# Turning a group's queries by DMA instead of by identity matmuls in a two-layer gated cross-attention kernel

## Chip, core and metric

The kernel runs on one core of a Trainium2 chip. The metric is the device time of one execution in microseconds (us), lower is better. The engines are named as in the profile: PE (TensorE matmuls) and PEld (its weight loads), DVE (VectorE), ACT (ScalarE), POOL (GpSimd) and SP (SyncE, which here only issues DMAs).

## What is computed

The input has 4 sequences of 256 tokens of width 256 and a context of 1601 rows each. Layer 0 is attention with two kinds of queries, a feed-forward part with eight experts follows, and layer 1 has another cross-attention and a product with weights made of bits. The change is in layer 0's attention, of which this is the core of the reference:

```
q  = _ln(linear_fp8(ln_out, wq ).reshape(b, s, g, hpg, d), qln_w,  qln_b)
k  = _ln(linear_fp8(ln_out, wk ).reshape(b, s, g, d), kln_w, kln_b)
core = _gqa(q, k, v)                       # over the 256 own tokens
qx = _ln(linear_fp8(ln_out, wqx).reshape(b, s, g, hpg, d), qxln_w, qxln_b)
xout = _gqa(qx, kx, vx)                    # over the 1601 context rows
catq = div_clamp_fp8(concat([core, xout]), proj_smooth)
out  = catq @ wproj.T * (proj_in_scale * proj_w_scale)
```

There are g = 8 groups with hpg = 2 heads of d = 128 each, so that a kind of query of one group and one sequence is 2 x 2 blocks (128 tokens x 128 features). `_ln` normalises over the 128 features of a head and then multiplies by a weight and adds a bias for each feature.

## The kernel before

**Turns.** Layer 0's attention is a loop of 32 turns, one for each pair of group and sequence (`NGB`, the variable `it`). Every engine runs an order written out by hand in a loop over `it` of its own (`pe_attention`, `act_attention`, `dve_attention`, `pool_attention`, `sp_attention`), with semaphores between them. In turn `it` the scores and the softmax of four blocks n = 4*it to 4*it+3 are made, while keys, queries and values of turn it+1 are prepared, and the products with V and the projection of earlier turns are finished. A score block n takes two steps on PE, `scores(n, 0)` and `scores(n, 1)` (L1810).

**Precision.** The two operands of each attention product are held as two bf16 tiles, an upper part and what it leaves (the lower part), and multiplied in three matmuls.

**Queries.** For each kind (i = 0 the cross kind, i = 1 the own kind) PE makes a block of 128 tokens x 512 (L1763, `queries`); DVE takes the statistics (L1249, L1255); POOL makes scale and shift (L1083 to L1088); ACT normalises four blocks into `kn` (L1509). PE then turns them, so that features lie on partitions, with four fp32 identity matmuls (L1774, `turn_queries`, two kinds a turn), since the scores need them so. ACT applies weight and bias, which are now per partition, while it reads PSUM (L1521, `query_full`, into `t32`, shown as `t`). POOL rounds to bf16 (L1097) and makes the lower part (L1099) in `QT` (`query_low`). `scores(4*it, 0)` and `scores(4*it, 1)` wait for these.

**Key row.** PE sums the keys' squares (L1711), ACT sends them to `ssc` (L1530, L1534), POOL takes their power in `key_norm` (L1108), and SP writes the row to memory (`row_out`, L987) and reads it back broadcast over the partitions (`row_in`, L1000, 936 KB, into `rsb` in odd turns and into `x` in even ones). DVE multiplies each score block by it (L1289).

**Probabilities.** ACT takes exponentials (L1555, L1556) and writes the upper part `PB` (L1565, `p_hi`), DVE the lower part (L1311, `p_lo`), POOL those of the own tokens (L1125, L1127, L1129, `split_self`). SP then turns each block of them by two transposing DMAs (L1015, `turn_p(n, h)`: half h = 0 is 16 tiles of 128 x 128 in bf16, half h = 1 is 14), eight a turn, and PE multiplies by V (L1830, `times_v`). `p_hi(n, h)` may write its half of `PB` only when that half of block n-2 has landed.

**SP's order in a turn.** Weights for later turns (L970) and pieces of other inputs; then `turn_p(4*it, 1)`, `turn_p(4*it, 0)`, `turn_p(4*it+1, 0)`; the key row out and in; the projection's weights (L978, 512 KB); `turn_p(4*it+1, 1)` and the last four `turn_p` of the turn. All DMAs of SP share one queue, whose 16 engines serve it in order.

## Times and profile before

| | |
|---|---|
| median of 3 runs | 1680.82 us (1679.46 to 1682.97) |
| profiled execution, first to last instruction | 1678.0 us |
| attention loop of layer 0, first to last score matmul | 61.0 to 1145.8 us |
| PE busy over the whole span | 1597.7 us, 95% |
| DVE, ACT, POOL busy | 1389.4, 1387.6, 1130.8 us |
| DMA queue of SP | 258.05 MB, 71.3% of 16 engines' time |

The profile has no time of its own for the profiled execution beside its span; the median of the plain runs is 2.8 us above that span, and this part (launch and end) is outside what the trace shows. In the profile's slices a digit is a busy share in tenths. A DMA share can exceed 1, since packets of one DMA engine overlap. In rows of the timeline a merged group's start and length are given, and in brackets the idle time ahead of it and what ended it.

### The profile page before, as it was taken

The page shows a single profiled execution, that of the slowest core. Times are in us where ns is not written, and L with a number is a line of the kernel's source. Part 1 is how long each engine was busy: PE and PEld are TensorE (multiplying, and loading weights), DVE is VectorE, ACT ScalarE, POOL GpSimd, SP SyncE. Part 2 cuts the span into 40 slices and gives each one's busy share as a digit, 9 for nine tenths or more (in the row PEclk, how much of TensorE's full clock was granted, in tenths as well). Part 3 has the DMA queues.
Part 4 walks back from the last instruction along what each step waited for, and adds up shares of the span by engine and source line. Part 5 has one row for each costly group of instructions (what it writes and reads, how often), then busy time and mean ns, then how long its engine had stood idle before and what let it go on. Part 6 is the DMA issues. An engine that isn't in the chain of part 4 may idle for free. (4 is left out here: it accounts for less than half of the span.)

```text
span 1678.0 us, 44059 instructions
## 1 busy us (share of the span) xinstructions
PE 1597.7 (95%) x15996; PEld 1003.1 (60%) x15996; DVE 1389.4 (83%) x3489; ACT 1387.6 (83%) x2340; POOL 1130.8 (67%) x1766
## 2 busy tenths in 40 slices
PE   3799999999999999999999999997898999999998
PEld 1476777767777677777777777765564333333333
DVE  7889999999999989999988999999896755655422
ACT  6688888888887888888887887876347999999997
POOL 3568778687787877888787878875575655646300
PEclk9799999999999999999999999998999999999999
DMA  5299989899989998999999999999323222222100
GB/s 179 85 200 204 195 196 198 188 203 208 211 193 202 223 206 187 213 223 220 206 198 215 220 220 192 201 189 237 95 48 115 46 46 74 45 40 46 33 14 14
DMA packets 608904, 261.11 MB, mean 156 GB/s; under 512 B 576560, under 2 KB 581680, under 8 KB 607280
## 3 DMA queue, kind: packets, MB, share of 16 engines
q1 hardware_dynamic: 604464, 258.05, 71.3%
q8 instruction: 127, 2.08, 0.5%
q10 hardware_dynamic: 4224, 0.25, 0.2%
q14 instruction: 89, 0.73, 0.1%
HBM read 99.15 MB, written 17.29 MB: 69 GB/s over the span
## 5 line engine op out<-in xcount | busy, mean ns | idle before, releaser
L1810 PE MATMUL score<-KK,QT 128*128 128x512 bf16 (+2 forms) x1920 | 341.8, 322 | 7.4 <-DVE mxp L1289 7.3
L1830 PE MATMUL pv<-PT,VV 128*128 128x256 bf16 (+1 forms) x2880 | 335.7, 273 | 6.1 <-DMA PT<-PB 6.1
L1565 ACT ACTIVATE PB<-S,rsum 128x1024 bf16<-128x1024 f32 (+1 forms) x256 | 246.3, 988 | 105.5 <-DVE rsum L1320 79.6
L1830 PEld LDWEIGHTS pv<-PT,VV 128*128 128x128 bf16 (+1 forms) x2880 | 278.3, 98 | 70.8 <-issue 31.6
L1311 DVE SCALAR_TENSOR_TENSOR PB<-S,rsum,PB 128x1024 bf16<-128x1024 f32 (+1 forms) x256 | 291.1, 1138 | 0.0
L1810 PEld LDWEIGHTS score<-KK,QT 128*128 128x128 bf16 x1920 | 157.9, 98 | 145.3 <-DVE mxp L1289 14.5
L1555 ACT ACTIVATE S<-S,nmx 128x1601 f32<-128x1601 f32 x128 | 210.1, 1641 | 3.6 <-DVE nmx L1301 3.5
L2870 ACT ACTIVATE P<-score 128x1024 f32<-128x1024 f32 x196 | 198.0, 1054 | 1.7 <-PE score L2962 0.8
L1689 PE MATMUL tb<-stage,wsb 128*128 128x512 bf16 (+1 forms) x768 | 149.5, 337 | 5.2 <-DVE stage L643 3.9
L2982 PE MATMUL pv<-P,V 128*9 128x256 f32 (+1 forms) x2288 | 152.2, 380 | 1.1 <-DVE pv L2253 0.8
L1125 POOL TENSOR_SCALAR S<-S,rsum 128x256 f32<-128x256 f32 x128 | 72.2, 564 | 115.3 <-DVE rsum L1320 107.4
L1147 POOL TENSOR_TENSOR catq<-yt,ym 128x512 bf16<-128x512 f32 x64 | 116.1, 1813 | 0.3
L1289 DVE CUSTOM_DVE_ANT_0 S<-score,x 128x1024 f32<-128x1024 f32 (+1 forms) x128 | 104.5, 816 | 7.5 <-PE score L1810 5.5
L1289 DVE CUSTOM_DVE_ANT_0 S<-score,rsb 128x1024 f32<-128x1024 f32 (+1 forms) x128 | 104.5, 816 | 6.7 <-PE score L1810 2.9
L1689 PEld LDWEIGHTS tb<-stage,wsb 128*128 128x128 bf16 x768 | 66.5, 98 | 71.3 <-issue 8.5
L1137 POOL TENSOR_TENSOR yt<-yq,ym 128x512 f32<-128x512 bf16 x64 | 94.8, 1482 | 12.8 <-DVE ym L1345 8.3
L1730 PE MATMUL tb<-wsb,stage 128*128 128x128 bf16 x1536 | 99.7, 223 | 3.0 <-DVE KK L1222 2.8
L1509 ACT ACTIVATE kn<-pa,a_nm,a_rs 128x128 f32<-128x128 f32 x256 | 95.5, 454 | 8.1 <-POOL a_nm L1088 8.0
L1083 POOL TENSOR_SCALAR a_nm<-a_mv 128x4 f32<-128x4 f32 x64 | 41.7, 651 | 89.3 <-DVE a_mv L1255 89.3
L1730 PEld LDWEIGHTS tb<-wsb,stage 128*128 128x128 bf16 x1536 | 94.1, 100 | 7.2 <-DVE KK L1222 5.2
L1481 ACT ACTIVATE KK<-tb,dcols 128x512 bf16<-128x512 f32 (+1 forms) x128 | 76.1, 594 | 25.7 <-PE tb L1689 25.7
L1129 POOL TENSOR_TENSOR PB<-S,PB 128x256 bf16<-128x256 f32 x128 | 89.3, 698 | 10.9
(293 smaller groups left out, 3679.6 us busy)
## 6 DMA issues: line engine op xcount, KB each, us to landing
x<-rs_d SPq DMA_DIRECT2D x16, 936.0 KB, 5.0
rsb<-rs_d SPq DMA_DIRECT2D x16, 936.0 KB, 5.6
wsb<-w_split SPq DMA_DIRECT2D x46, 256.0 KB, 4.7
wsb<-w_split SPq DMA_DIRECT2D x23, 512.0 KB, 4.8
wpr<-in_wprojT SPq DMA_DIRECT2D x23, 512.0 KB, 6.5
context_d<-stage SPq DMA_DIRECT2D x16, 400.2 KB, 3.8
l_ctx<-context_d SPq DMA_DIRECT2D x4, 1601.0 KB, 7.8
rawh<-in_w_all SPq DMA_DIRECT2D x12, 512.0 KB, 5.8
```

Source lines behind the costliest of these rows:

```text
L1147: e.tensor_tensor(out[:, :, pr * 256:(pr + 1) * 256], m.yt[:, :].rearrange("p (k c) -> p k c", k=2), m.ym[pr][:, :].rearrange("p (k c) -> ...
L1289: e.tensor_tensor_reduce(m.S32[par][:, at:at + b - a], m.score[:, a:b], m.rsb[it % 2][:, key:key + b - a], 1.0, start, ALU.mult, ALU.max, ...
L1311: e.scalar_tensor_tensor(m.PB[n % 2][:, lo:lo + b - a], m.S32[n % 2][:, a:b], m.rsum[n % 2][:, 1:2], m.PB[n % 2][:, 2 * a:a + b], ALU.mult ...
L1509: a = e.activation(m.kn[i][:, k * D:(k + 1) * D], bank[:, k * D:(k + 1) * D], ACT.Identity, bias=m.anm[i][:, k:k + 1], scale=m.ars[i][:, k ...
L1555: e.activation(x, x, ACT.Exp, bias=m.nmx[par][:, 1:2], accum_out=m.sums[par][:, 1:2])
L1565: e.activation(m.PB[n % 2][:, 2 * a:a + b], m.S32[n % 2][:, a:b], ACT.Copy, scale=m.rsum[n % 2][:, 1:2]).then_inc(s["p_hi"], 1)
L1689: r = e.matmul(bank[:, 0:b - a], wk[:, w, ic, D:2 * D], ctx_op(m, it, part, ic, a, b), start=(n == 0), stop=(n == 5))
L1730: r = e.matmul(bank[:, h * D:(h + 1) * D], ctx_op(m, it, part, ic, t * P, (t + 1) * P), wv[:, w, ic, D:2 * D], start=(n == 0), stop=(n == 5))
L1810: i = e.matmul(m.score[:, at:at + b - a], qt[:, kind, qp, q * P:(q + 1) * P], kk[:, kp, a:b], start=(k == 0), stop=(k == 2))
L1830: i = e.matmul(m.pv[:, at:at + 256], vv[0:rows, v, t, :], m.PT[k % 2][0:rows, turned(c, a), :], start=(c == first and r == 0), stop=(c == ...
L2870: e.activation(pr[:, :], bank, ACT.Exp, scale=float(D1) ** -0.5).then_inc(s["l1_exp"], 1)
L2982: r = e.matmul(m.pv[j * R:j * R + VC, 0:S], m.V1[p][0:rows, t, 4 * hq + j, :], probabilities(m, n, j // 2)[0:rows, at:at + S], start=(t == ...
```

## The change

The eight identity matmuls of a turn go, and ACT's pass with weight and bias over PSUM with them. Weight and bias now lie along the free dimension (`qrow`, the four vectors broadcast to all partitions by one DMA at the start), and POOL applies them to `kn` in two instructions (`query_weighted`). ACT writes the upper part in bf16 (`query_high`), POOL the lower part (`query_low`), both into `q16`, and SP turns upper and lower part of a kind in one transposing DMA of 8 tiles (`turn_q`) into `QT`. `kn` is one buffer instead of two. The slots of PSUM banks that the turned queries had are left empty.

```diff
@@ -193,8 +193,9 @@
             m.wsb = sb(c, "wsb", [P, 2 * IC * WCOLS], BF16)
             m.sq = sb(c, "sq", [P, SQG * SQW], F32)
             m.sqs = sb(c, "sqs", [P, SQW], F32)
-            m.kn = [sb(c, f"kn{i}", [P, 512], F32) for i in range(2)]
-            m.t32 = sb(c, "t32", [P, 512], F32)
+            m.kn = sb(c, "kn", [P, NQ, D], F32)
+            m.qrow = sb(c, "qrow", [P, 4, D], F32)
+            m.q16 = sb(c, "q16", [P, 2, NQ * D], BF16)
             qt, kk, vv = [None, None], [None, None], [None, None]
             qt[0] = sb(c, "QT0", [P, 2, 2, NQ * P], BF16)
             kk[0] = sb(c, "KK0", [P, 2, KCOLS], BF16)
...
@@ -506,6 +507,7 @@
     e.dma_start(m.cols[:, :], A["cols"]).then_inc(s["const_in"], 16)
     e.dma_start(m.dcols[:, :], A["dcols"]).then_inc(s["const_in"], 16)
     e.dma_start(m.scal[:, :], A["scal"].partition_broadcast(P)).then_inc(s["const_in"], 16)
+    e.dma_start(flat(m.qrow[:, :, :]), A["qrow"].partition_broadcast(P)).then_inc(s["const_in"], 16)
     e.dma_start(m.smc[:, :], A["smooth"]).then_inc(s["const_in"], 16)
     sp_load_weights(e, m, s, 0)
     sp_load_context(e, m, s, 0, 0)
...
@@ -838,8 +840,8 @@
 
 
 
-SLOTS = (("Q0",), ("K0",), ("K1",), ("TQ0",), ("K2",), ("K3",), ("Q1",), ("SS",), ("V0",), (), ("V1",), ("TQ1",), ("V2",),
-         ("V3",), ("PR",))
+SLOTS = (("Q0",), ("K0",), ("K1",), (), ("K2",), ("K3",), ("Q1",), ("SS",), ("V0",), (), ("V1",), (), ("V2",), ("V3",),
+         ("PR",))
 ORDER = tuple(w for slot in SLOTS for w in slot)
 SLOT = {w: n for n, slot in enumerate(SLOTS) for w in slot}
 LAG = 3
...
@@ -1014,6 +1014,15 @@
             e.wait_ge(s["tv_done"], 2 * (k - 2) + h + 1)
         e.dma_start_transpose(m.PT[k % 2][:, 2 * a // P:2 * b // P, (n % 2) * P:(n % 2 + 1) * P],
                               m.PB[n % 2][:, 2 * a:2 * b]).then_inc(s[f"pt{h}_in{n % 2}"], 16)
+
+    def turn_q(it, i):
+        if not it < NGB:
+            return
+        e.wait_ge(s["q_lo"], 2 * it + i + 1)
+        if it >= 2:
+            e.wait_ge(s["bank_full"], 8 * (it - 1))
+        e.dma_start_transpose(m.QT[it % 2][:, 1 - i, :, :].rearrange("p a (k q) -> p (a k) q", q=P),
+                              flat(m.q16[:, :, :])).then_inc(s["qt_in"], 16)
 
     for it in range(-1, NGB + LAG - 1):
         if it == -1:
...
@@ -1045,6 +1054,7 @@
         load_weights(it + 2, 0)
         if it + 2 >= PAIRS:
             load_weights(it + 2, 1)
+        turn_q(it + 1, 0)
         turn_p(4 * it, 1)
         turn_p(4 * it, 0)
         turn_p(4 * it + 1, 0)
...
@@ -1056,6 +1066,7 @@
             load_projection(it - 1)
         if it == NGB - 1:
             load_projection(NGB - 1)
+        turn_q(it + 1, 1)
         turn_p(4 * it + 1, 1)
         if it == NGB - 2:
             load_projection(it - 1)
...
@@ -1087,17 +1098,25 @@
         e.wait_ge(s["rs_pow"], 2 * c + 2)
         e.tensor_tensor(m.anm[i][:, :], m.anm[i][:, :], m.ars[i][:, :], ALU.mult).then_inc(s["nm_done"], 1)
 
+    def query_weighted(it, i):
+        if not it < NGB:
+            return
+        c, w = 2 * it + i, 2 * (1 - i)
+        if c == 0:
+            e.wait_ge(s["const_in"], 80)
+        e.wait_ge(s["normed"], c + 1)
+        e.tensor_tensor(m.kn[:, :, :], m.kn[:, :, :], m.qrow[:, w:w + 1, :].broadcast_to([P, NQ, D]),
+                        ALU.mult).then_inc(s["q_t32"], 1)
+        e.wait_ge(s["q_t32"], 2 * c + 1)
+        e.tensor_tensor(m.kn[:, :, :], m.kn[:, :, :], m.qrow[:, w + 1:w + 2, :].broadcast_to([P, NQ, D]),
+                        ALU.add).then_inc(s["q_t32"], 1)
+
     def query_low(it, i):
         if not it < NGB:
             return
-        c, kind = 2 * it + i, 1 - i
-        e.wait_ge(s["q_t32"], c + 1)
-        if it >= 2:
-            e.wait_ge(s["bank_full"], 8 * (it - 1))
-        e.tensor_copy(m.QT[it % 2][:, kind, 0, :], m.t32[:, :]).then_inc(s["q_hi"], 1)
+        c = 2 * it + i
         e.wait_ge(s["q_hi"], c + 1)
-        e.tensor_tensor(m.QT[it % 2][:, kind, 1, :], m.t32[:, :], m.QT[it % 2][:, kind, 0, :],
-                        ALU.subtract).then_inc(s["q_lo"], 1)
+        e.tensor_tensor(m.q16[:, 1, :], flat(m.kn[:, :, :]), m.q16[:, 0, :], ALU.subtract).then_inc(s["q_lo"], 1)
 
     def key_norm(it):
         if not it < NGB:
...
@@ -1151,18 +1170,19 @@
         if it == 0:
             e.wait_ge(s["xq_done"], 8)
             for i in range(2):
-                e.memset(m.S32[i][:, SC:SELFC], 0.0).then_inc(s["p_pad"], 1)
+                e.memset(m.S32[i][:, SC:SELFC], 0.0).then_inc(s["set_zero"], 1)
         query_norm(it + 1, 0)
         take_magnitudes(2 * it - 3)
         split_self(4 * it - 1)
+        query_weighted(it + 1, 0)
         if it < NGB - 1:
             projection_low(it - 2)
         if it == -1:
             pool_context_low(e, m, s, 1, 0)
             pool_context_low(e, m, s, 1, 1)
+        query_low(it + 1, 0)
         split_self(4 * it)
         query_norm(it + 1, 1)
-        query_low(it + 1, 0)
         if it == -1:
             pool_split_weights(e, m, s, 1, 0)
             pool_round_end(e, m, s, 4)
...
@@ -1170,11 +1190,12 @@
         if 0 <= it < SPLITS and it % 2 == 0:
             pool_split_weights(e, m, s, it // 2 + 2, 1)
         split_self(4 * it + 1)
+        query_weighted(it + 1, 1)
         key_norm(it + 1)
         if it == -1:
             pool_round_end(e, m, s, 5)
+        query_low(it + 1, 1)
         add_magnitudes(2 * it - 2)
-        query_low(it + 1, 1)
         if it == -1:
             pool_round_end(e, m, s, 6)
         if it == NGB - 4:
...
@@ -1503,23 +1524,21 @@
             return
         bank = bank_of(m, f"Q{i}")
         e.wait_ge(s["nm_done"], 2 * it + i + 1)
-        if it:
-            e.wait_ge(s["pa_full"], made(it - 1, f"TQ{i}"))
+        if it or i:
+            e.wait_ge(s["q_lo"], 2 * it + i)
         for k in range(NQ):
-            a = e.activation(m.kn[i][:, k * D:(k + 1) * D], bank[:, k * D:(k + 1) * D], ACT.Identity,
+            a = e.activation(m.kn[:, k, :], bank[:, k * D:(k + 1) * D], ACT.Identity,
                              bias=m.anm[i][:, k:k + 1], scale=m.ars[i][:, k:k + 1])
         a.then_inc(s["normed"], 1)
 
-    def query_full(it, i):
+    def query_high(it, i):
         if not it < NGB:
             return
-        c, kind = 2 * it + i, 1 - i
-        w = ("qln", "qxln")[kind]
-        e.wait_ge(s["pa_full"], made(it, f"TQ{i}"))
+        c = 2 * it + i
+        e.wait_ge(s["q_t32"], 2 * c + 2)
         if c:
-            e.wait_ge(s["q_lo"], c)
-        e.activation(m.t32[:, :], bank_of(m, f"TQ{i}")[:, :], ACT.Identity, scale=dcol(m, w + "_w"),
-                     bias=dcol(m, w + "_b")).then_inc(s["q_t32"], 1)
+            e.wait_ge(s["qt_in"], 16 * c)
+        e.copy(m.q16[:, 0, :], flat(m.kn[:, :, :])).then_inc(s["q_hi"], 1)
 
     def sums_out(it):
         if not it < NGB:
...
@@ -1592,7 +1611,7 @@
                 act_norm_weighted(e, m, s, ic)
             act_scaled_inputs(e, m, s, 4)
         exponentials(4 * it)
-        query_full(it + 1, 0)
+        query_high(it + 1, 0)
         for j in SCALES_AT.get(it, ()):
             act_scaled_inputs(e, m, s, j)
         act_piece_high(e, m, s, it, "A")
...
@@ -1641,7 +1660,7 @@
             for what, c in ffn_slots(0):
                 act_prepare(e, m, s, 0, what, c)
         values_high(it + 1, 1)
-        query_full(it + 1, 1)
+        query_high(it + 1, 1)
         act_piece_high(e, m, s, it, "D")
         if 0 <= it < SPLITS:
             act_weights_high(e, m, s, it // 2 + 2, 3 * (it % 2))
...
@@ -1764,16 +1783,6 @@
                              wq[:, w, ic, kind * 256:(kind + 1) * 256], start=(n == 0), stop=(n == 3))
         r.then_inc(s["pa_full"], 1)
 
-    def turn_queries(it, i):
-        if not it < NGB:
-            return
-        bank = bank_of(m, f"TQ{i}")
-        wait_bank(e, s, it, f"TQ{i}")
-        e.wait_ge(s["normed"], 2 * it + i + 1)
-        for k in range(NQ):
-            r = e.transpose(bank[:, k * P:(k + 1) * P], m.kn[i][:, k * D:(k + 1) * D], m.ident[:, :])
-        r.then_inc(s["pa_full"], 1)
-
     def project(i):
 
         if not 0 <= i < NGB:
...
@@ -1798,7 +1807,7 @@
         if q == 0:
             if half == 0:
                 e.wait_ge(s["k_lo"], 4 * it + 4)
-            e.wait_ge(s["q_lo"], 2 * it + 1 + half)
+            e.wait_ge(s["qt_in"], 16 * (2 * it + 1 + half))
         if n and half == 0:
             e.wait_ge(s["mm"], 3 * (n - 1) + 1)
         elif n:
...
@@ -1841,7 +1850,6 @@
             pe_turn_normed(e, m, s, 1)
         scores(4 * it + 1, 0)
         times_v(2 * it - 2, 1)
-        turn_queries(it + 1, 0)
         scores(4 * it + 1, 1)
         keys(it + 1, 2)
         keys(it + 1, 3)
...
@@ -1864,7 +1872,6 @@
         if it != NGB - 1:
             scores(4 * it + 2, 1)
         values(it + 1, 1)
-        turn_queries(it + 1, 1)
         values(it + 1, 2)
         values(it + 1, 3)
         scores(4 * it + 3, 0)
...
@@ -3110,6 +3117,7 @@
     names = ["ln_w", "ln_b", "q_in_scale", "qx_in_scale", "k_in_scale", "v_in_scale"]
     out["cols"] = np.ascontiguousarray(np.concatenate([l0(n).reshape(IC, P).T for n in names], axis=1))
     out["dcols"] = np.ascontiguousarray(np.stack([l0(n) for n in DCOLS], axis=1))
+    out["qrow"] = np.concatenate([l0(n) for n in ("qln_w", "qln_b", "qxln_w", "qxln_b")])
     out["scal"] = np.concatenate([z.reshape(-1) for z in (
         l0("wq_scale"), l0("wqx_scale"), l0("wk_scale"), l0("wv_scale"), l0("proj_w_scale"), l0("proj_in_scale"),
         a["g_xattn"], a["g_ffn"], a["L1_ffn_scale"], a["L1_ffn_biasscale"])])
```

On SP, this is one turn before, from the key row of one turn to the last transposes ahead of the next one (`rs_d<-rr` is the row out, `PT<-PB` a `turn_p`).

```order
L987 DMA rs_d<-rr 128x15 [waits rs_in0,kr_pow]
L1000 DMA x<-rs_d 128x1872 [waits mm,rs_row]
L978 DMA wpr<-in_wprojT 128x1024 [waits pw_lo]
L1015 DMA_TRANSPOSE PT<-PB 128x14x128 [waits tv_done,s_lo,p_lo]
L1015 DMA_TRANSPOSE PT<-PB 128x16x128 [waits tv_done,p_lo]
```

And the same place in the changed program.

```order
L987 DMA rs_d<-rr 128x15 [waits rs_in0,kr_pow]
L1000 DMA x<-rs_d 128x1872 [waits mm,rs_row]
L978 DMA wpr<-in_wprojT 128x1024 [waits pw_lo]
L1024 DMA_TRANSPOSE QT<-q 128x8x128 [waits bank_full,q_lo]
L1015 DMA_TRANSPOSE PT<-PB 128x14x128 [waits tv_done,s_lo,p_lo]
L1015 DMA_TRANSPOSE PT<-PB 128x16x128 [waits tv_done,p_lo]
```

The own kind's queries (i = 1) are turned behind the key row and the projection's weights and ahead of the last five `turn_p`. Also on SP, this is the place before between the last `turn_p` of one turn and the first ones of the next.

```order
L1015 DMA_TRANSPOSE PT<-PB 128x14x128 [waits tv_done,s_lo,p_lo]
L970 DMA wsb<-w_split 128x1024 [waits pa_full]
L484 DMA stage<-inputs_d 128x2048 [waits xq_out1,xq_out0,ctx_lo_dve]
L970 DMA wsb<-w_split 128x1024 [waits pa_full]
L970 DMA wsb<-w_split 128x2048 [waits pa_full]
L1015 DMA_TRANSPOSE PT<-PB 128x14x128 [waits tv_done,s_lo,p_lo]
```

And in the changed program.

```order
L970 DMA wsb<-w_split 128x1024 [waits pa_full]
L485 DMA stage<-inputs_d 128x2048 [waits xq_out1,xq_out0,ctx_lo_dve]
L970 DMA wsb<-w_split 128x1024 [waits pa_full]
L970 DMA wsb<-w_split 128x2048 [waits pa_full]
L1024 DMA_TRANSPOSE QT<-q 128x8x128 [waits bank_full,q_lo]
L1015 DMA_TRANSPOSE PT<-PB 128x14x128 [waits tv_done,s_lo,p_lo]
```

The cross kind's queries (i = 0) are turned behind the weights and ahead of `turn_p(4*it, 1)`.

On POOL, this is the stretch before from the second query's statistics to the magnitudes (`a_nm`, `a_rs` are shift and scale, `S`, `PB` the own tokens' probabilities, `rr` the key row).

```order
L1088 TENSOR_TENSOR a_nm<-a_nm,a_rs 128x4 [waits rs_pow]
L1097 CAST QT<-t 128x512 [waits bank_full,q_t32]
L1099 TENSOR_TENSOR QT<-t,QT 128x512 [waits q_hi]
L1125 TENSOR_SCALAR S_1<-S_1,rsum 128x256 [waits pt1_in1,sum_read]
L1127 CAST PB<-S_1 128x256 [waits s_hi]
L1129 TENSOR_TENSOR PB<-S_1,PB 128x256 [waits s_hi]
L1108 TENSOR_TENSOR rr<-ssc,mhalf 128x15 [waits rs_row,sums_in]
L1137 TENSOR_TENSOR yt<-yq,ym 128x512 [waits yq_done,y_mag]
L1097 CAST QT<-t 128x512 [waits bank_full,q_t32]
L1099 TENSOR_TENSOR QT<-t,QT 128x512 [waits q_hi]
```

And the same stretch of the changed program.

```order
L1099 TENSOR_TENSOR a_nm<-a_nm,a_rs 128x4 [waits rs_pow]
L1144 TENSOR_SCALAR S_1<-S_1,rsum 128x256 [waits pt1_in1,sum_read]
L1146 CAST PB<-S_1 128x256 [waits s_hi]
L1148 TENSOR_TENSOR PB<-S_1,PB 128x256 [waits s_hi]
L1108 TENSOR_TENSOR kn<-kn,qrow 128x512 [waits normed]
L1111 TENSOR_TENSOR kn<-kn,qrow 128x512 [waits q_t32]
L1127 TENSOR_TENSOR rr<-ssc,mhalf 128x15 [waits rs_row,sums_in]
L1119 TENSOR_TENSOR q<-kn,q 128x512 [waits q_hi]
L1156 TENSOR_TENSOR yt<-yq,ym 128x512 [waits yq_done,y_mag]
```

The two new instructions of the own kind stand ahead of the key row's power, and the cross kind's cast and lower part no longer stand in this stretch (its new ones are earlier in the turn).

## Rows read from the trace of the kernel before

**Rows 1.** The page: busy time of the engines, DMA share in 40 slices.

```profile
PE 1597.7 (95%) x15996; PEld 1003.1 (60%) x15996; DVE 1389.4 (83%) x3489; ACT 1387.6 (83%) x2340; POOL 1130.8 (67%) x1766
DMA  5299989899989998999999999999323222222100
```

**Rows 2.** Busy time by stretch: length, PE, PEld, DVE, ACT, POOL, PEclk, DMA share, GB/s.

```profile
306.90:343.00 36.10, 35.91 (x324) 25.95 (x323) 34.19 (x86) 30.13 (x57) 27.91 (x32) 1.00 0.95 198
818.30:852.35 34.05, 34.05 (x314) 25.06 (x313) 30.09 (x80) 28.15 (x53) 27.39 (x31) 1.00 0.97 206
920.50:954.55 34.05, 34.05 (x315) 25.06 (x313) 31.68 (x82) 28.36 (x51) 28.18 (x31) 1.00 1.02 219
```

**Rows 3.** Timeline of PE, 818 to 863 us: start, length, line, out<-in, count.

```profile
818.54 1.46 PE L1810 MATMUL score<-KK,QT 128*128 128x512 bf16 x6
...
842.42 0.60 PE L1774 MATMUL tb<-ident,kn 128*128 128x128 f32 x4
842.86 1.50 PE L1730 MATMUL pa<-wsb,stage 128*128 128x128 bf16 x24
...
852.59 1.46 PE L1810 MATMUL score<-KK,QT 128*128 128x512 bf16 x6
...
855.19 1.24 PE L1810 MATMUL score<-KK,QT 128*128 128x512 bf16 x9
```

**Rows 4.** The page's groups of POOL: count, busy us, mean ns, idle before.

```profile
L1137 POOL TENSOR_TENSOR yt<-yq,ym 128x512 f32<-128x512 bf16 x64 | 94.8, 1482 | 12.8 <-DVE ym L1345 8.3
L1099 POOL TENSOR_TENSOR QT<-t,QT 128x512 bf16<-128x512 f32 x64 | 76.9, 1201 | 5.2
L1097 POOL CAST QT<-t 128x512 bf16<-128x512 f32 x64 | 42.9, 670 | 0.2 <-issue 0.2
```

**Rows 5.** Timeline of POOL, 838 to 848 us.

```profile
841.72 2.75 POOL L1108 TENSOR_TENSOR rr<-ssc,mhalf 128x15 f32<-128x15 f32 x1
...
846.63 1.16 POOL L1099 TENSOR_TENSOR QT<-t,QT 128x512 bf16<-128x512 f32 x1
```

**Rows 6.** Timeline of ACT, 821 to 858 us.

```profile
821.34 0.69 ACT L1481 ACTIVATE KK<-tb,dcols 128x512 bf16<-128x512 f32 x1 [0.35 <-PE tb L1689]
...
838.80 1.48 ACT L1509 ACTIVATE kn<-pa,a_nm,a_rs 128x128 f32<-128x128 f32 x4
...
857.39 0.84 ACT L1565 ACTIVATE PB<-S,rsum 128x640 bf16<-128x640 f32 x1
```

**Rows 7.** Timeline of SP, 831 to 872 us: a length is how long SP was held by the issue.

```profile
831.08 2.14 SPq L970 DMA_DIRECT2D wsb<-w_split  x2
837.03 7.85 SPq L1015 DMA_TRANSPOSE PT<-PB  x3
844.98 0.98 SPq L987 DMA_DIRECT2D rs_d<-rr  x1
847.57 0.32 SPq L1000 DMA_DIRECT2D rsb<-rs_d  x1
...
848.47 14.39 SPq L1015 DMA_TRANSPOSE PT<-PB  x5
```

**Rows 8.** DMAs issued at 847.57 and 848.47 us: size, us from issue to landing.

```profile
rsb<-rs_d SPq DMA_DIRECT2D x1, 936.0 KB, 6.1
PT<-PB SPq DMA_TRANSPOSE x1, 8.2
```

**Rows 9.** The `turn_p(4*it+1, 1)` issued at 917.56 us: us to landing.

```profile
PT<-PB SPq DMA_TRANSPOSE x1, 9.0
```

**Rows 10.** Busy time by stretch, columns as in Rows 2.

```profile
836.50:838.00 1.50, 1.50 (x15) 1.34 (x14) 1.37 (x2) 0.82 (x2) 1.34 (x4) 1.00 0.24 98
...
846.50:848.50 2.00, 2.00 (x20) 1.61 (x19) 1.81 (x5) 1.01 (x6) 1.22 (x2) 1.00 0.16 25
...
853.00:864.60 11.60, 11.60 (x83) 7.16 (x82) 10.08 (x28) 9.64 (x17) 8.95 (x10) 1.00 1.15 227
...
869.50:872.00 2.50, 2.50 (x24) 1.55 (x24) 2.28 (x5) 1.36 (x5) 2.20 (x5) 1.00 0.21 74
```

28 lines of the change are left out of this document (13 added, 15 removed).

## The prediction

> **What bounds the kernel now.** I read the page first. PE is busy 95% of the span, and the DMA engines stand at 9 tenths in most slices of the attention loop [rows 1]. Then the busy time by stretch. In the two turns from 818 and from 920 us PE is busy all of 34.05 us at full clock, VectorE 30 to 32, ScalarE 28, GpSimd 27 to 28, and the DMA share is 0.97 and 1.02 [rows 2]. So PE sets these turns: one goes from the score matmul at 818.54 to that at 852.59 [rows 3], 34.05 us. Some turns are different: in 306.9 to 343.0 PE and VectorE (34.19 of 36.10) are both nearly full [rows 2]. By the same reading five of the 32 turns are held by VectorE. I call the others PE's; the early ones among them take some 0.4 us more than 34.05 and get the same treatment.
>
> **What goes.** Four identity matmuls run from 842.42 to the next block at 842.86 [rows 3]: 0.44 us (their length of 0.60 overlaps what follows). Two kinds a turn make 0.88 us, and 32 turns 28.2 us. The trace shows no idle PE in these turns to swallow that. ScalarE's pass with weight and bias becomes a copy of the same 128x512, no dearer; I cost this edit at nothing, since ScalarE has 6 us free a turn [rows 2]. The floor is therefore 1680.8 - 28.2 = 1652.6 us, with a PE turn of 33.17.
>
> **What comes on GpSimd.** Per kind two 128x512 operations in fp32 come and one cast of 0.67 goes; the lower part of 1.20 stays. No row has two fp32 inputs and an fp32 output at this width. The nearest are 1.20 (fp32 and bf16 in) and 1.48 (fp32 out) [rows 4]; I take 1.25, the inputs counting more, with both as ends. That is 2 x (2 x 1.25 - 0.67) = 3.7 us a turn (3.5 to 4.6): GpSimd goes from 27 or 28 to 31 or 32 of 34 us [rows 2], still below PE. What matters is where they stand. The key row's power ran at 841.72 to 844.47 [rows 5]. In the new order it stands behind the own kind's two operations, which wait for ScalarE's normalised block at 838.80 + 1.48 = 840.28 [rows 6]: 840.3 + 2.5 + 2.75 = 845.5, so 1.1 us later. SP issued the row at 844.98 [rows 7], so its issue slips by 0.6. Half of this is hidden, for the row out can only land behind the transposes already queued; I take 0.3 us for the row's return. The lower part then ends at 845.5 + 1.2 = 846.7, before SP comes to it at 848.47 [rows 7].
>
> **What comes on the DMA queue.** Two transposes of 8 tiles. Their rate is that of the busy stretch 853.0 to 864.6, at 227 GB/s [rows 10]: 128 x 1024 x 2 bytes = 262 KB take 1.15 us; the five `turn_p` there are 74 tiles in 11.6 us [rows 7, 10], or 1.25 for 8 tiles. I take 1.2 each, 2.4 a turn. A table of the Trainium skill (VectorE: DVE Perf Modes, "Rules for kernel authors") says to turn a 128x128 tile on TensorE if PSUM will do as the place, and by DMA otherwise, at 1309 ns a tile by DMA. That rule speaks against this change. By its figure 16 tiles would be an estimated 21 us a turn, but here 8 tiles take 1.2, so the figure is that of a lone tile and the sum goes by the rows.
>
> *The cross kind* is issued while SP waits: its last load is out at 833.2 and the next `turn_p` goes at 837.03 [rows 7]. The DMA engines are at 0.24 from 836.5 to 838 and at 0.21 from 869.5 to 872 [rows 10]. There it costs nothing. In turns with more loads this gap is full, and all behind it comes up to 1.2 us later.
>
> *The own kind* stands behind the key row, which lands at 847.57 + 6.1 = 853.7, and behind the projection's weights. `turn_p(4*it+1, 1)` landed at 848.47 + 8.2 = 856.7 from that place [rows 7, 8]. It has 14 tiles, so 8 tiles would land 6 x 0.15 = 0.9 earlier, at 855.8. PE wants them for the second half of the first score block at 855.19 [rows 3]: 0.6 us too late. In the turn with the 917.56 issue the landing took 9.0 [rows 9], to 926.6, less 0.9 is 925.7. PE's time there is 855.19 plus two turns, 923.29: 2.4 late. I take 1.2 for a mean over turns, plus 0.3 for the row, plus 0.3 for filled gaps: 1.8 us.
>
> **Three loops that must shorten for a gain.** (a) Queries. The chain to this landing starts at ScalarE's run from 821.34, which follows PE's first keys [rows 6], ahead of the place where PE would now wait. A late landing so delays the chain only through the turn after, and two turns share it: period = 34.05 + (1.8 - 0.88)/2 = 34.5. With 0.6 late in place of 1.8 it is 33.9; with 2.4 + 0.3 + 1.2 it is 35.6. (b) Probabilities. `turn_p(4*it+1, 1)` landed at 856.7 and ScalarE writes that buffer again at 857.39 [rows 6]: 0.7 in hand. In the other turn it landed at 926.6, where ScalarE wants it at 857.39 plus two turns, 925.5: 1.1 late, and PE was still full from 920.5 on [rows 2, 9]. So 1.8 is in hand at least. It gets 1.2 + 0.3, and up to 1.2 more: 33.8 to 35.0. (c) The queue itself. From 836.5 to 872 it is idle in three places: 1.1 us, 1.7 us and 2.0 us [rows 10]. The first and the last are the same place of two turns, so one counts. The 1.7 us is the round trip of the key row, for which SP waits, and stays. So some 2.0 of a light turn can be filled, and 2.4 come: 34.4. All three centre on 34.4 or above, and none comes near 33.17.
>
> **Sum.** I take 34.45, that is +0.4 us for 24 turns (+9.6), nothing for the five of VectorE, and the full gain for three at the edges (-2.6): +7. Against the profiled span of 1678.0 that is 1685, against the median 1688. Measurement tells nothing apart within 0.2% (3.4 us).
>
> **Rivals.** *PE's saving comes through.* For it: PE is truly full, and rows show idle in every other queue. Loop (a) would have to be under 33.2, which takes a landing some 2.4 us earlier than I find, for instance if transposes of 8 tiles in one piece run much faster or the key row comes earlier. Full: 1653 to 1664. Chance 0.13. *Half of it comes:* a period of 33.7, just under the low ends of (a) and (b), gives 1680.8 - 24 x 0.35 - 2.6 = 1670; 1664 to 1677. Chance 0.16. *It does nothing:* the loops come out at 34.05, within 1677.4 to 1684.2. Chance 0.14. *Slower, as forecast:* 1684 to 1712, chance 0.50. *The queue becomes the bound everywhere:* early turns and the one from 920 us (share 1.02) have no gap to fill; then 2.4 - 0.5 = 1.9 us come to 24 turns, less the edges: 1724. Chance 0.07. For loop (b) or a full VectorE a rule of the Trainium skill would matter too (GPSIMD Engine Reference, "Key points": GpSimd shares its SBUF interfaces with VectorE where that reads two SBUF inputs). It has no price there, and VectorE's 2 to 4 us free a turn cover a third of a microsecond for each new instruction.
>
> **Numbers.** Predicted 1688. Leaving out most of the two outer cases gives 1664 to 1712; the slower case's own range is 1684 to 1712. Faster 0.29, same 0.14, slower 0.57.
>
> **What would show it.** PE should wait ahead of the second score half of each turn for `QT<-q16`, about 1 us, and ScalarE's `PB` at the turn's start for `PT<-PB`. The key row should be issued some 0.5 us later within a turn, and the turn should be 34.3 to 34.7 us with PE's busy time down by 0.88. GpSimd's new operations should take 1.2 to 1.5 us. I am wrong if PE stays full at 33.2 us a turn, or if the own kind's landing comes before the second score half.

## The result and the profile after

The changed kernel takes 1753.88 us (median of 4 runs, 1752.87 to 1757.86), the kernel before 1680.16: ratio 1.0438, 95% interval 1.0421 to 1.0454. That is slower by 73.7 us, where 7 were forecast, and outside the range. The profiled execution spans 1752.6 us.

The page of the changed kernel, its busy times, DMA digits and queue:

```profile
PE 1587.0 (91%) x15740; PEld 975.1 (56%) x15740; DVE 1423.7 (81%) x3489; ACT 1379.6 (79%) x2340; POOL 1232.6 (70%) x1830
...
DMA  4399999999999999999999999989443223222200
...
q1 hardware_dynamic: 672192, 275.10, 75.7%
```

Against [rows 1] PE has lost 10.7 us of work, ScalarE 8, GpSimd has gained 101.8. VectorE was not touched, and yet it is busy 34.3 us longer.

Two neighbouring turns, in the columns of [rows 2]; the first begins where the score matmul at 869.04 does:

```profile
869.04:904.46 35.42, 33.75 (x306) 24.08 (x304) 33.10 (x80) 27.79 (x53) 29.93 (x33) 1.00 1.07 207
904.46:939.88 35.42, 33.52 (x306) 24.11 (x304) 30.91 (x79) 27.06 (x50) 29.10 (x33) 1.00 1.04 214
```

The clock is full (1.00), as before. PE now has 1.7 to 1.9 us idle in a light turn, and no engine is busy for the whole turn. These two are among the shortest turns: from one first score matmul to the next it is 36.4 us in the mean (34.3 before), and 41.2 in the longest. Over all turns the first score matmul is at 66.4 and the last at 1221.0 us, so the attention loop is 69.8 us longer than before and starts 5.4 later.

PE's timeline at the start of two turns, to be held against [rows 3]:

```profile
904.46 1.46 PE L1819 MATMUL score<-KK,QT 128*128 128x512 bf16 x6
905.76 1.46 PE L1708 MATMUL tb<-stage,wsb 128*128 128x512 bf16 x6
909.05 1.14 PE L1819 MATMUL score<-KK,QT 128*128 128x512 bf16 x8 [1.83 <-DMA QT<-q]
...
943.60 1.25 PE L1819 MATMUL score<-KK,QT 128*128 128x512 bf16 x9 [0.97 <-DMA QT<-q]
```

The second score half waits for the own kind's landing, at the place foretold; the waits are 1.83 and 0.97 us, where about 1 was foretold. The key row, though, goes out later than was reckoned. This is SP's issue of it in the second of the two turns:

```profile
933.85 0.32 SPq L987 DMA_DIRECT2D rs_d<-rr  x1
```

That is 29.4 us into its turn; in [rows 7] it is 844.98, 26.4 us into the turn from 818.54. Over 31 turns the mean is 30.6 us against 27.7, so 2.9 us later, where 0.6 was forecast.

The table of waits (who waited for whom: us in total, times, longest) shows more than that, though:

```profile
ACT PB L1584 <- DVE rsum L1341: 109.4, 87, 3.0
...
POOL S L1144 <- DVE rsum L1341: 54.0, 57, 3.2
PE score L1819 <- DMA QT<-q: 51.4, 29, 3.3
...
ACT q L1541 <- POOL kn L1111: 41.1, 43, 1.9
...
ACT PB L1584 <- DMA PT<-PB: 33.1, 29, 2.6
```

In the kernel before the first two were 79.6 and 107.4 us. So GpSimd used to wait 107 us for the reciprocals and now waits 54, while ScalarE waits 30 us longer for the same reciprocals: they come later, and GpSimd comes to them later still. The groups of POOL and then of DVE, for the whole run:

```profile
L1108 POOL TENSOR_TENSOR kn<-kn,qrow 128x512 f32<-128x512 f32 x64 | 96.8, 1512 | 20.4 <-ACT kn L1530 20.3
...
L1111 POOL TENSOR_TENSOR kn<-kn,qrow 128x512 f32<-128x512 f32 x64 | 82.3, 1286 | 5.0
L1119 POOL TENSOR_TENSOR q<-kn,q 128x512 bf16<-128x512 f32 x64 | 76.3, 1192 | 11.6 <-ACT q L1541 11.6
```

```profile
L1361 DVE TENSOR_SCALAR yq<-yq 128x512 bf16<-128x512 bf16 x64 | 47.3, 739 | 0.1
L1363 DVE TENSOR_SCALAR ye<-yq 128x512 int16<-128x512 int16 x64 | 40.8, 637 | 2.2
L1366 DVE TENSOR_SCALAR ym<-ye 128x512 int16<-128x512 int16 x64 | 21.5, 336 | 2.2
```

The new GpSimd operations have the size foretold (1.2 to 1.5 us). VectorE's three small operations of `exponents` took 422, 367 and 296 ns before, and now 739, 637 and 336: 40 us more in all, which is more than the 34.3 us by which VectorE's busy time grew. They stand in VectorE's queue right ahead of the reciprocal `rsum`.

It is mostly not the new operations that run beside them. Taking 294 ns as their undisturbed length, the three were 53 us over it in the changed kernel (13 before). By the GpSimd instruction that overlaps each longest, 19 us of this stand beside the queries' lower part (L1119), 16 beside the sum `yt` (L1156), 15 beside the projection's lower part (L1133), and only 2.0 beside the new sum (L1111). In e8 below, with the changed order but without the weighting, the first three are 18, 0 and 3 us. So the lower part came there by the changed order, and the other two were pushed there by the new operations.

### The profile page after: what moved, and what is told of

The parts are those of the page before. It is cut to its first block, busy times and chain, and to the rows that moved or that the text cites. A ratio compares the mean times of both kernels' runs of the same rounds, so it can differ in the third digit from the quotient of the medians.

```text
span 1752.6 us, 43614 instructions
## 1 busy us (share of the span) xinstructions
PE 1587.0 (91%) x15740; PEld 975.1 (56%) x15740; DVE 1423.7 (81%) x3489; ACT 1379.6 (79%) x2340; POOL 1232.6 (70%) x1830
## 4 chain that ended last, share of the span: by engine, by line
PE 28%; DVE 8%; DMA 7%; issue 5%; ACT 5%; POOL 2%; SPq 1%; ACTq 0%; DVEq 0%; POOLq 0%
PE pv L2989 9%; DMA QT<-q 4%; PE pa L2939 4%; PE pv L1839 4%; PE score L1819 3%; PE score L2969 2%; ACT P L2877 2%; PE tb L1708 1%; DMA rs_d<-rr 1%; POOL rr L1127 1%; PE tb L2969 1%; ACT praw L2877 1%; DVE S L1310 1%; PE pv L2177 1%; DMA PT<-PB 1%
## 5 line engine op out<-in xcount | busy, mean ns | idle before, releaser
L1819 PE MATMUL score<-KK,QT 128*128 128x512 bf16 (+2 forms) x1920 | 346.5, 325 | 53.9 <-DMA QT<-q 51.4
L1819 PEld LDWEIGHTS score<-KK,QT 128*128 128x128 bf16 x1920 | 158.1, 99 | 201.2 <-DMA QT<-q 66.4
L1144 POOL TENSOR_SCALAR S<-S,rsum 128x256 f32<-128x256 f32 x128 | 65.1, 509 | 72.7 <-DVE rsum L1341 54.0
L1108 POOL TENSOR_TENSOR kn<-kn,qrow 128x512 f32<-128x512 f32 x64 | 96.8, 1512 | 20.4 <-ACT kn L1530 20.3
L1148 POOL TENSOR_TENSOR PB<-S,PB 128x256 bf16<-128x256 f32 x128 | 93.5, 731 | 10.9
L1156 POOL TENSOR_TENSOR yt<-yq,ym 128x512 f32<-128x512 bf16 x64 | 88.6, 1385 | 16.8 <-DVE ym L1366 12.3
L1502 ACT ACTIVATE KK<-tb,dcols 128x512 bf16<-128x512 f32 (+1 forms) x128 | 75.4, 589 | 31.1 <-PE tb L1708 30.6
```

What stands on the lines that cost most here:

```text
L1108: e.tensor_tensor(m.kn[:, :, :], m.kn[:, :, :], m.qrow[:, w:w + 1, :].broadcast_to([P, NQ, D]), ALU.mult).then_inc(s["q_t32"], 1)
L1819: i = e.matmul(m.score[:, at:at + b - a], qt[:, kind, qp, q * P:(q + 1) * P], kk[:, kp, a:b], start=(k == 0), stop=(k == 2))
```

## The experiments

Theory 1 at the start was the prediction's own loop (a): the late landing, but not shared by two turns. Its rivals were ScalarE's wait for GpSimd (A), contention of GpSimd with VectorE (B), GpSimd's queue itself (C), and the bytes on the DMA queue. The first six expectations speak of theory 1 and of numbered rivals and say what each holds; from e7_pool_casts on they use the letters. All times below are medians; ratios are against the kernel before on the same chip, with their 95% interval.

| run | us | ratio |
|---|---|---|
| e1_no_dma | 1730.27 | 1.0290 [1.0275, 1.0305] |
| e2_no_wait | 1745.93 | 1.0389 [1.0370, 1.0408] |
| e3_before_weights | 1743.42 | 1.0362 [1.0346, 1.0377] |
| e4_key_first | 1812.82 | 1.0771 [1.0753, 1.0789] |
| e5_cross_by_dma | 1722.12 | 1.0239 [1.0224, 1.0255] |
| e6_own_by_dma | 1735.26 | 1.0312 [1.0278, 1.0346] |
| e7_pool_casts | 1735.98 | 1.0333 [1.0314, 1.0352] |
| e8_no_weight | 1679.47 | 0.9995 [0.9985, 1.0004] |
| e9_extra_ops | 1768.15 | 1.0527 [1.0511, 1.0543] |
| e10_extra_scalar_ops | 1804.49 | 1.0739 [1.0723, 1.0755] |
| e11_extra_pow | 1731.47 | 1.0298 [1.0283, 1.0314] |
| e12_first_only | 1705.93 | 1.0145 [1.0130, 1.0160] |
| e13_second_only | 1720.58 | 1.0238 [1.0221, 1.0255] |
| e14_behind_key | 1766.79 | 1.0507 [1.0491, 1.0523] |
| e15_matmuls_out | 1680.17 | 0.9993 [0.9983, 1.0002] |
| e16_act_casts | 1687.64 | 1.0035 [1.0022, 1.0047] |
| e17_short_loads | 1676.50 | 0.9971 [0.9960, 0.9983] |
| e18_short_exponents | 1669.33 | 0.9927 [0.9907, 0.9948] |

### The transfers

**e1_no_dma.** From the changed kernel: no transposing DMA of queries, and the scores read a tile of zeros, so that nothing waits for a landing.

```diff
-        turn_q(it + 1, 0)
-        turn_q(it + 1, 1)
-            e.wait_ge(s["qt_in"], 16 * (2 * it + 1 + half))
+            e.wait_ge(s["q_lo"], 2 * it + 1 + half)
```

> The changed kernel without its transposing DMAs: the scores read a tile of zeros in place of the turned queries, so no PE instruction waits for a landing and the queue carries what it carried before; all of the new work of GpSimd and ScalarE stays, and the identity matmuls stay out. Theory 1 (the loop through the own kind's landing sets the turn, one turn long): the turn falls to PE's 33.2 to 33.6 us, 1653 to 1668 in all. Rival 2 (GpSimd's two added operations a kind, and their contention with VectorE, are the loss): it stays above 1700.

1730.27. Transfer and wait together are worth 23.6 us of the 73.7. The other 50 come without any transfer of queries, so theory 1 falls as the main cause; the time lies in rival 2's range.

**e2_no_wait.** All transfers but the first turn's stay, and only the wait is moved: the scores read zeros, and the landing is awaited at the fourth score block.

```diff
+        if q == 3 and half == 0 and it:
+            e.wait_ge(s["qt_in"], 16 * 2 * it)
```

> The changed kernel with all its DMAs, but the scores of all turns but the last read a tile of zeros, and the landing is only awaited three score blocks later. The queue's load and order are those of the changed kernel. Theory 1 (latency of the own kind's landing): most of the loss goes, 1665 to 1700. Rival 3 (the DMA queue is full, its throughput sets the turn): it stays at 1730 to 1755.

1745.93. So the bytes on the queue alone cost 15.7 us (over e1), and the wait for them 8.0 (to the changed kernel), though the trace counts 51.4 us of PE's wait. The 8.0 hold a second thing, since ScalarE's wait for the last landing before it writes `q16` is put off by a turn as well. A wait of PE is not a loss of its length: most of that time is not won back when the wait goes.

**e3_before_weights.** The own kind's transfer goes ahead of the projection's weights.

```diff
         row_in(it + 1)
+        turn_q(it + 1, 1)
         ...
-        turn_q(it + 1, 1)
```

> The changed kernel with one line of SP moved: the own kind's transpose is issued right behind the key row's return and ahead of the projection's weights (512 KB). Theory 1 (one-turn loop through this landing): the landing comes some 1.5 to 2 us earlier in the turns that load these weights, and the turn shortens by as much until another loop holds: 1710 to 1730. Rival 3 (throughput of the queue): no change, within 5 us of the changed kernel.

1743.42, 10.5 us better: PE's wait fell to 18.2 us. The time lies in neither expectation (1710 to 1730, or within 5 us of the changed kernel). This is the whole change with a better place, and still 61 us slower than before.

**e4_key_first.** GpSimd raises the key row before it weights the own kind.

```diff
-        query_weighted(it + 1, 1)
         key_norm(it + 1)
+        query_weighted(it + 1, 1)
```

> The changed kernel with one line of GpSimd moved: the key row's power stands ahead of the own kind's weight and bias, as it stood before in the order of work. Theory 1: the key row goes out 2.8 us earlier and comes back so much earlier, the own kind's lower part ends about when it did (30.8 us into the turn), so its transpose is issued 1 to 2 us earlier: 1715 to 1735. Rival 3: no change. Rival 2 (amount of GpSimd work): no change.

1812.82, the worst of all. ScalarE's cast stands in the middle of ScalarE's order and now waits for the bias behind a 2.75 us power: `ACT q` waited for `POOL kn` 158.6 us, 60 times, in place of 41.1. So the wait of theory A can be expensive where it is long. It says nothing yet of the 41.1.

**e5_cross_by_dma and e6_own_by_dma.** One kind by the new way, the other by identity matmuls as before, both through the one tile `kn`.

```diff
-        query_weighted(it + 1, 1)        # e5; in e6: (it + 1, 0)
-        turn_q(it + 1, 1)
+        turn_queries(it + 1, 1)          # TensorE
```

> Only the cross kind is turned by DMA (with GpSimd's weight and bias), the own kind goes by four identity matmuls and ScalarE as before. Theory 1: the cross kind lands some 11 us before it is wanted, so the long wait is gone; PE keeps half of its saving, less what the shared kn buffer and GpSimd cost: 1665 to 1690. Rival 3 (queue full): half of the loss, about 1715. Rival 2 (GpSimd): half of the loss too.

> Only the own kind is turned by DMA, the cross kind goes by identity matmuls as before. Theory 1: nearly all of the loss stays, 1730 to 1755, with PE waiting 1 to 2 us a turn for the landing. Rivals 2 and 3: half of the loss, about 1715.

1722.12 and 1735.26. The cross kind, which was to be free, costs 41 us; no PE wait for its landing is among its long waits. Each half has one pair of GpSimd's weighting operations. The two together (41.5 and 54.7) are more than the whole change. In e6 there is a wait that neither whole kernel has: GpSimd's cast of the cross kind waited 55.8 us for ScalarE's weighting pass, which goes through the shared `kn`. So e6 overstates its half.

### GpSimd

**e7_pool_casts.** e1 with its scores of zeros, and GpSimd makes the bfloat16 cast too, so that ScalarE waits for GpSimd no more.

```diff
-        query_high(it + 1, 0)            # ScalarE, and (it + 1, 1)
+        e.tensor_copy(m.q16[:, 0, :], flat(m.kn[:, :, :])).then_inc(s["q_hi"], 1)
```

> The kernel of the run without the query transfers (1730.3 us), and there GpSimd also makes the bfloat16 cast of the queries, so that ScalarE no longer waits for GpSimd's two weighting operations; ScalarE loses 2 casts of 0.62 us a turn, GpSimd gains 2 of 0.4 to 1.5 us. Theory A (ScalarE's in-order wait between GpSimd's bias and its own cast delays the exponentials and copies behind it, 64.4 us of waits in that run): 1695 to 1712 us. Theory B (GpSimd's added two-input operations stretch VectorE's bfloat16 scalar operations, 0.29 us to over 1 us, and so the reciprocals): 1725 to 1745, since GpSimd does no less. Theory C (GpSimd's own queue is late with the key row's power, 0.1 of which a turn would be the casts too): 1735 or more.

1735.98, 5.7 us above e1 and not 20 to 35 below it. As the main cause theory A falls. But the run changes two things at once: ScalarE no longer waits (64.4 us in e1) and has 33 us less work, and GpSimd has 43 us more (1282.6 busy against 1239.8). ScalarE's wait for the reciprocals went from 113.2 to 193.0 us. Added GpSimd work costs 0.3 to 0.5 us for each microsecond in e9 to e11, so an estimate is that the 43 us cost 12 to 22, and that what ScalarE was spared gave 7 to 17 back. That those waits are worth nothing isn't shown.

**e8_no_weight.** e1 without the weighting operations; weight and bias of the queries are left out.

```diff
-        query_weighted(it + 1, 0)
-        query_weighted(it + 1, 1)
-        e.wait_ge(s["q_t32"], 2 * c + 2)
+        e.wait_ge(s["normed"], c + 1)
```

> The kernel of the run without the query transfers (1730.3 us), and there without GpSimd's two weighting operations a group: ScalarE casts the normed queries as they are, GpSimd only subtracts. It leaves out weight and bias of the queries, and the scores read a tile of zeros as in that run. All theories that lay the remaining 50 us on the four new GpSimd operations a turn (waits, contention or queue) expect the time that the removed identity matmuls give: 1650 to 1668 us. If it stays above 1690, the loss lies elsewhere: in the shared tile of normed queries or in the new cast on ScalarE.

1679.47. The four operations of a turn, with ScalarE's wait for them, are worth 50.8 us, all of what e1 left over the kernel before. The expected further gain, down to 1650 to 1668, didn't come, although the identity matmuls are gone here too.

**e9_extra_ops.** The other way round: the kernel before, with a product and a sum on a scratch tile put where the changed kernel weights the queries. Nothing reads them.

```diff
+        e.tensor_tensor(m.dm[:, :, :], m.dm[:, :, :], row, ALU.mult).then_inc(s["dm_in"], 1)
+        e.wait_ge(s["dm_in"], 2 * c + 2)
+        e.tensor_tensor(m.dm[:, :, :], m.dm[:, :, :], row, ALU.add).then_inc(s["dm_in"], 1)
```

> The kernel before, its identity matmuls kept, with only GpSimd's two-input operations added: at the two places where the changed kernel weights the queries, a 128x512 float32 product and a sum on a scratch tile that nothing reads, behind the same wait for the normed queries. Nobody waits for their results. Theory A (ScalarE waits for GpSimd): within 12 us of before, 1680 to 1695. Theory B (contention with VectorE's fast operations): 1705 to 1735, with the bfloat16 scalar operations of VectorE stretched as in the changed kernel. Theory C (GpSimd's queue alone): 1705 to 1735 without stretched VectorE operations.

1768.15: 87.6 us for four operations that nobody waits for, more than the whole change and more than any theory expected (the kernel before also has its two casts on GpSimd). GpSimd's timeline here shows no gap above 0.15 us from 904.36 to 932.48. Three of its rows:

```profile
928.94 1.41 POOL L1101 TENSOR_TENSOR dm<-dm,ident 128x512 f32<-128x512 f32 x1
930.31 2.17 POOL L1127 TENSOR_TENSOR wpb<-wpr,wpb 128x1024 bf16<-128x1024 f32 x1
...
946.32 2.74 POOL L1121 TENSOR_TENSOR rr<-ssc,mhalf 128x15 f32<-128x15 f32 x1
```

and VectorE's timeline beside them:

```profile
929.26 1.24 DVE L1357 TENSOR_SCALAR ye<-yq 128x512 int16<-128x512 int16 x1
930.53 2.10 DVE L1360 TENSOR_SCALAR ym<-ye 128x512 int16<-128x512 int16 x1
932.56 0.15 DVE L1335 RECIPROCAL rsum<-sums 128x2 f32<-128x2 f32 x1
...
948.33 0.29 DVE L1357 TENSOR_SCALAR ye<-yq 128x512 int16<-128x512 int16 x1
948.66 0.29 DVE L1360 TENSOR_SCALAR ym<-ye 128x512 int16<-128x512 int16 x1
948.87 0.16 DVE L1335 RECIPROCAL rsum<-sums 128x2 f32<-128x2 f32 x1
```

The same two VectorE instructions take 0.29 us each while GpSimd raises to a power, and end only behind GpSimd's instruction where that moves a full tile: 1.24 us from 929.26 on, beside a GpSimd instruction that ends at 930.35, and 2.10 from 930.53 on, beside one that ends at 932.48. The reciprocal behind them is 2.7 us late.

**e10_extra_scalar_ops.** As e9, each pair as six one-input operations.

```diff
+        for k in range(6):
+            e.wait_ge(s["dm_in"], 6 * c + k + 1)
+            e.tensor_scalar(m.dm[:, :, :], m.dm[:, :, :], 1.0, 1.0, ALU.mult, ALU.mult).then_inc(s["dm_in"], 1)
```

> As the run with GpSimd's added two-input operations, but each pair is six one-input operations of the same tile (about 0.48 us each, so as long in sum). Theory B, if the contention is between two-input operations and VectorE: well under that run, 1680 to 1695, and VectorE's bfloat16 scalar operations near their 0.29 us. Theory C (GpSimd's queue alone): the same time as that run within 6 us. If VectorE's operations are stretched here as well, the contention asks for no second input.

1804.49. The operations were longer than reckoned (mean 0.68 us, so GpSimd gained 265 us and not 168), and VectorE's instructions beside them took 0.67. The contention asks for no second input. Per added microsecond on GpSimd the loss is 0.47, near that of e9 (87.6 of 168, 0.52).

**e11_extra_pow.** As e9, but the four operations raise 128x6 numbers to a power: as long, and almost without data.

```diff
+        e.tensor_tensor(m.dm[:, 1, 0:6], row, m.mhalf[:, 0:6], ALU.pow).then_inc(s["dm_in"], 1)
```

> The kernel before with GpSimd occupied at the same two places of a turn, but by operations that move next to no data: each of the four added operations raises 128x6 numbers to a power (from the 1.02 us of 128x4 and 2.75 us of 128x15, about 1.33 us each, as long as the two-input operations of the run that cost 87.6 us). Theory C (GpSimd's queue: what stands behind the added operations comes later, the key row above all, and the turn closes over it): 1745 to 1775, as that run. Theory B (VectorE and GpSimd slow each other down where both move data): 1680 to 1705, with VectorE's operations at their lengths of before. Half and half: 1710 to 1740.

1731.47: 50.2 us for 172.6 us more on GpSimd, against e9's 87.6 for 167.6. That is the "half and half" of the expectation. An occupied GpSimd without much data costs 50, and the data moved another 37. The queue by itself is worth 50 at most, and the contention 37 at least, since even here VectorE's work grew by 40 us (1429.6 busy): other GpSimd operations were pushed beneath its instructions, and `ym<-ye` took 554 ns on average.

**e12_first_only and e13_second_only.** One of the two pairs of e9.

```diff
         extra(it + 1, 0)
-        extra(it + 1, 1)                 # e12; e13 leaves out the other
```

> The kernel before with the added pair of two-input GpSimd operations at the first place of the turn only (behind the first split_self, 27 us ahead of the key row's power). Theory C by the key row: the pair is absorbed in GpSimd's waits of that stretch, 1680 to 1700. Theory B (contention alone): half of the 87.6 us, 1715 to 1735.

> The kernel before with the added pair at the second place only (between the third split_self and the key row's power, which so comes 2.7 us later). Theory C by the key row: most of the 87.6 us, 1740 to 1765. Theory B (contention alone): half, 1715 to 1735.

1705.93 and 1720.58: 24.6 and 39.3 us. The second place is dearer, the two together (87.6) dearer than their sum (63.9). e13 lies in the range of B, e12 in neither. That fits a first pair which takes what free time GpSimd has ahead of its waits, so that the second finds less; the traces don't prove it.

**e14_behind_key.** As e9, the second pair behind the key row's power and the lower part.

```diff
-        extra(it + 1, 1)
         key_norm(it + 1)
         ...
         query_low(it + 1, 1)
+        extra(it + 1, 1)
```

> The kernel before with both pairs, the second behind the key row's power and the second group's low part, so that GpSimd has as many operations in a turn as in the run that cost 87.6 us, but the key row is not behind the second pair. Theory C by the key row: 1680 to 1710. Theory C by the whole of GpSimd's time (it has no idle time left at all): 1755 or more, the place makes no difference. Theory B (contention alone): 1745 to 1770, the place makes no difference either.

1766.79, 85.5 us over the kernel before of its own chip, where e9 had 87.6. So a key row that stands behind the second pair is not the cause by itself (1680 to 1710 was expected for that). The sum hides a difference, though: VectorE is busy 1507.7 us here and 1480.6 in e9, and its three small operations are 129 us over 294 ns each, against 73 in e9. The same loss with so much more stretch says two things. What the place saves and what it costs may cancel, and the stretch summed over the run is no measure of the loss. e12 and e13 say so too: 68 us of stretch with a loss of 24.6, and 42 with 39.3.

### TensorE's saving

**e15_matmuls_out.** The kernel before, identity matmuls out, nothing in their place; ScalarE weights the rows unturned, so the scores are of another product of the same shape.

```diff
-        turn_queries(it + 1, 0)
-        turn_queries(it + 1, 1)
-        e.wait_ge(s["pa_full"], made(it, f"TQ{i}"))
+        e.wait_ge(s["normed"], c + 1)
```

> The kernel before with its eight identity matmuls a turn taken out and nothing put in their place: ScalarE's weighting pass reads the normed rows themselves, so the queries are not turned and the scores are of another product of the same shape. GpSimd, VectorE and the transfers keep their work. The prediction's floor (28.2 us less TensorE work, all of it through): 1650 to 1656. Rival, that the turn of before is held as long by the loop through GpSimd and VectorE as by TensorE (the run without the weighting operations gained 1.1 us only): 1672 to 1682.

1680.17: 0.9 us better, within the noise. PE's busy time fell by 18.9 us, and not by 28.2. Four turns in a row, in the columns of [rows 2]:

```profile
820.42:853.83 33.41, 33.35 (x306) 24.17 (x304) 30.08 (x81) 28.38 (x53) 27.36 (x31) 1.00 0.96 207
853.83:887.24 33.41, 33.34 (x307) 24.18 (x304) 29.73 (x80) 28.04 (x51) 27.01 (x31) 1.00 1.02 211
887.24:921.58 34.34, 33.67 (x307) 24.05 (x305) 30.56 (x80) 28.36 (x52) 27.30 (x32) 1.00 1.02 209
921.58:956.93 35.35, 33.67 (x307) 24.04 (x305) 30.64 (x80) 27.27 (x47) 26.76 (x30) 1.00 1.06 227
```

The first two turns take 33.4 us, 0.64 less than 34.05, where the prediction hoped for 0.88 less. The next two give it back: the four take 136.5 us, and 4 x 34.05 is 136.2. In the last one PE's timeline has

```profile
937.24 2.78 PE L1828 MATMUL pv<-PT,VV 128*128 128x256 bf16 x24 [1.49 <-DMA PT<-PB]
```

a wait for the probabilities' transposes that the kernel before doesn't show between 920 and 955 us. What PE gained in two turns it waits for in the next two. The DMA share is 1.06 in the last, but it is 1.02 both in a fast and in a slower one, so it doesn't tell by itself which turn is held.

These four are not the rule for the whole loop. Compared turn by turn, 8 of the 31 from one first score matmul to the next have 33.4 or 33.5 us, and seven of these are among the last ten, which together are 3.1 us shorter than before. One turn, 716.05 to 750.10 before and 715.64 to 752.67 here, gives 3.0 back: VectorE was busy 33.56 of its 34.05 us, and PE, now earlier, waits 1.81 us in it for VectorE's lower part of the keys. And the early turns of 34.4 us gain nothing, as the next runs show.

**e16_act_casts.** The kernel before, complete, with 36.8 us of work moved off GpSimd: ScalarE writes the queries' upper part itself, by a second pass over the bank, and waits until the earlier scores have freed that tile.

```diff
+        e.activation(m.QT[it % 2][:, kind, 0, :], bank_of(m, f"TQ{i}")[:, :], ACT.Identity,
+                     scale=dcol(m, w + "_w"), bias=dcol(m, w + "_b")).then_inc(s["q_t32"], 1)
-        e.tensor_copy(m.QT[it % 2][:, kind, 0, :], m.t32[:, :]).then_inc(s["q_hi"], 1)
```

> The kernel before with 42.9 us of work taken off GpSimd: ScalarE writes the queries' upper part itself by a second pass over the same bank (about 0.6 us twice a turn more on ScalarE), GpSimd only subtracts. If GpSimd's time counts by about half, as the added operations did, and ScalarE's is hidden: 1655 to 1672. If TensorE alone bounds the kernel before: 1679 to 1683. If ScalarE's added passes count: 1685 or more.

1687.64, slower by 6.6 us. GpSimd only waits longer for the reciprocals (145.3 us in place of 107.4), 37.9 us more for 36.8 less work. So the time freed on GpSimd went into waiting; what it was worth is not separated from what 36.5 us more on ScalarE cost. That fits a GpSimd that was just short of being late in the kernel before, so that less work gives little and more work costs.

**e17_short_loads and e18_short_exponents.** Both from e15. e17 moves only 64 columns of each reload of the split weights (23 MB less in all), and later groups use the first ones' weights. e18 leaves VectorE's clip and mask out of `exponents` (36 us less on VectorE).

```diff
-        a, b = w_at[which], w_at[which + 1]                # e17
+        a, b = w_at[which], w_at[which] + 64
```

```diff
-        e.tensor_scalar(y[:, :], y[:, :], FP8_MAX, -FP8_MAX, ALU.min, ALU.max).then_inc(s["clipped"], 1)  # e18
-        e.tensor_scalar(m.ye[:, :].bitcast(I16), y[:, :].bitcast(I16), 0x7F80, None,
-                        ALU.bitwise_and).then_inc(s["y_exp"], 1)
```

> The kernel before with the identity matmuls out (that run: 1680.2 us, no gain), and there the reloads of the split weights cut to 64 of their columns, so that about 1 MB a group is not moved and the weights of the first groups stay in use. If the transfers hold the turn of 34.0 us (their share is 0.9 to 1.0 in every turn): 1640 to 1660, TensorE's floor or a little above. If the loop through GpSimd and VectorE holds it: 1672 to 1681.

> The kernel before with the identity matmuls out (1680.2 us), and there two of VectorE's three small operations on each smoothed block left out (the clip and the mask; the magnitudes are made straight from the block), 50 us of VectorE's work in all, right ahead of a reciprocal that GpSimd and ScalarE wait for. If the loop from the reciprocal through GpSimd and ScalarE holds the turn: 1640 to 1665. If the transfers hold it: 1675 to 1681.

0.9971 and 0.9927, against e15's 0.9993: 3.7 us from the queue, 11 from VectorE. Neither alone gives the 28 back. One early turn, the same in the kernel before, e15, e17 and e18, in the columns of [rows 2]:

```profile
404.68:439.10 34.42, 34.23 (x315) 24.95 (x313) 32.52 (x86) 31.59 (x69) 28.87 (x35) 1.00 1.01 214
404.03:438.44 34.41, 33.69 (x306) 24.04 (x304) 32.50 (x86) 31.64 (x69) 28.88 (x35) 1.00 0.96 211
402.98:437.41 34.43, 33.31 (x301) 24.03 (x305) 32.52 (x86) 31.66 (x69) 28.89 (x35) 1.00 0.90 195
399.57:433.34 33.77, 33.13 (x301) 24.08 (x305) 31.26 (x81) 31.27 (x69) 29.26 (x36) 1.00 0.99 211
```

and PE in e15's turn:

```profile
409.59 1.47 PE L1808 MATMUL score<-KK,QT 128*128 128x512 bf16 x6 [0.43 <-DVE mxp L1287]
```

Less work on PE leaves its length as it was, fewer bytes do too, and less work on VectorE takes 0.65 us off it. Of such turns (34.41 to 34.47 us before) there are seven; together they take 241.1, 241.1, 241.2 and 238.5 us in the four kernels. So they were held by the path through VectorE and not by PE. The removed TensorE time is covered in at least two ways: by VectorE in these early turns, and in the late ones by single turns in which PE waits for the probabilities' transposes or for VectorE.

## Why the prediction was wrong

Its sign was right, its size was not: two terms failed, the floor and the price of GpSimd's new work, and a third, the transfers, came out near.

- **The floor, "PE saves 0.88 a turn, 28.2 us, and so 1652.6".** Failed. The work did go, though less of it (PE 1578.8 us busy in e15, 1597.7 before), but alone it is worth 0.9 us. The step "So PE sets these turns" was drawn from a full engine. In the late turns of 34.05 us it is partly right: seven of the last ten fall by 0.64 us. It failed most clearly for the early ones, which "get the same treatment": seven turns of 34.4 us stay as they are in e15 and shorten only in e18, with less work on VectorE.
- **"GpSimd goes to 31 or 32 of 34 us, still below PE", priced by the key row alone at 0.3 us.** Failed, and this is the step with which the forecast leaves its range. The size of the operations was right (1.51 and 1.29 us for 1.25), and GpSimd's busy time grew by 3.2 us a turn (3.7 forecast), but free time in a turn is not slack. Four operations a turn cost 50.8 us in the changed kernel (e1 less e8, with ScalarE's wait for them): 1.6 us a turn where 0.3 was counted. The key row went out 2.9 us later and not 0.6. But by e14 its place by itself is not the cause: the whole of GpSimd's order comes later, by e11 at a price of up to 50 us for four operations of 1.4 us.
- **"VectorE's 2 to 4 us free a turn cover a third of a microsecond for each new instruction."** Failed too. The contention was named without a price, and only for VectorE instructions that read two inputs; those measured here read one. It doesn't lengthen every instruction a little. It holds back a few by the whole length of GpSimd's instruction (1.24 and 2.10 us in place of 0.29), and those stand ahead of the reciprocal for which ScalarE and GpSimd both wait. By e9 against e11, data that GpSimd moves cost at least 37 us of 88 on the kernel before. That this goes by way of the reciprocals is read from the traces, and no run shows it by itself.
- **ScalarE "at nothing".** Not settled. Its waits for GpSimd went up by 41.1 us; e7, without them, is no faster, but has more GpSimd work. e4 shows the price if they grow.
- **"The cross kind costs there nothing."** Not settled for the transfer alone. Its whole edit costs 41 us (e5), and that holds one pair of GpSimd's operations.
- **Loop (a).** The mean landing was to be 1.8 us late; the trace shows 51.4 us in 29 waits, 1.8 each. What it costs is at most 8.0 us (e2), 0.25 a turn; +0.46 over PE's turn was taken for it.
- **Loop (c), the queue.** 16 to 24 us for 17 MB more (e2 and the changed kernel over e1), 0.5 to 0.7 a turn, near the +0.4 that was taken. In part that is luck. The +0.4 was 2.4 us of transfers less 2.0 of gaps in a turn of 34.05, while the measured price was paid in turns of about 36 us, and no run checks the gaps.

If the parts add, the forecast reads so afterwards: the floor is e8's 1679.5 (the matmuls out, no weighting, no transfers), the transfers bring it to about 1703, which lies within the stated range, and GpSimd's weighting brings it to 1754.

What stays open: how the 50 us of the changed kernel's weighting divide between queue and contention (e9 and e11 divide them on the kernel before only), and whether the wait of ScalarE has a share in them. A version of the weighting that keeps clear of VectorE's small operations wasn't tried. None of the complete kernels here (e3 to e6, e16) beats the kernel before.

## What to carry to other kernels

An engine that is full is not the only limit of a tuned loop: take its work out and give nothing in return once (e15) before counting the saving, and look at the turns one by one, since they can have different limits. Work added to an engine "with 6 us free" is charged by what stands behind it, here 0.3 to 0.5 of its length, so look where its waits are and not how long they are in all. On GpSimd ask also which short VectorE instructions then run beside its work, the old work that is pushed along included, and who waits behind them.

## What the runs showed of the hardware

VectorE's 128x512 int16 operations with one input (two of `exponents`) over six traces (before, changed, e1, e9, e10, e11), sorted by what GpSimd ran in their first 250 ns (other rare cases and those with two GpSimd operations in that time are left out):

```
GpSimd at that time                    count   median ns (min to max)
nothing                                  342    294  (293 to 298)
power, 128x6 or 128x15                   141    294  (293 to 295)
one-input product, 128x512 fp32           74    667  (586 to 672)
cast to bf16, 128x512                     25    580  (579 to 582)
difference, 128x512 (before, e9, e11)     22   1202  (1155 to 1208)
difference, 128x512 (changed, e1)         50   1128  (293 to 1295)
sum `yt` to fp32, 128x512                 32   1124  (1117 to 1128)
added product or sum, 128x512 fp32         8   1243  (1237 to 1246)
difference to bf16, 128x1024              38   2100  (2096 to 2112)
```

Of the 263 that began beside a single data-moving GpSimd instruction, 248 ended 0.14 to 0.16 us behind its end. 13 took 294 ns, all beside the difference in the changed kernel and e1, and they had begun together with it or up to 0.22 us ahead of it. The Trainium skill (SBUF — State Buffer, "SBUF: two separate sides") says this: the two share one pair of ports by an exclusive lock that is held for a whole instruction, for a VectorE operation in a 2-port mode or with two SBUF inputs. The trace agrees for the operations that move a full tile. For the power it doesn't: 141 VectorE operations ran at 294 ns beside it, so a GpSimd instruction of 1.3 to 2.8 us doesn't hold VectorE back merely by running.

It was also new that a wait of PE counted at 51.4 us was worth at most 8.0 (e2).
